# A four-layer decoder on one core: the expert router of layer 2 picks its 64 tokens by quarters and numbers them with matmuls

## What is computed

```python
xf = x.reshape(n_tokens, d)                       # 1024 x 128
rms = jnp.sqrt(jnp.mean(xf * xf, axis=-1, keepdims=True) + EPS)
xn = xf / rms * norm_weight
logits = xn @ router_weight.T + router_bias       # 1024 x 16
probs = jax.nn.softmax(logits, axis=-1)
_, idx = jax.lax.top_k(logits.T, top_k)           # 16 x 64, top_k = 1024 / 16
xe = xn[idx]
h = jnp.einsum('ecd,efd->ecf', xe, fc1_weight) + fc1_bias[:, None, :]
h = jax.nn.gelu(h, approximate=False)
y = jnp.einsum('ecf,edf->ecd', h, fc2_weight) + fc2_bias[:, None, :]
gates = jnp.take_along_axis(probs.T, idx, axis=1)
flat_idx = idx.reshape(-1)
contrib = (y * gates[:, :, None]).reshape(-1, d)
output = jnp.zeros((n_tokens, d), dtype=x.dtype).at[flat_idx].add(contrib)
gate_sums = jnp.zeros((n_tokens, 1), dtype=x.dtype).at[flat_idx].add(gates.reshape(-1, 1))
```

## Time and profile before

| | us |
|---|---|
| runs before | 1656.31, 1650.27, 1657.39 |
| median | 1656.31 |
| profiled execution, its own time | 1656.52 |
| its span in the trace | 1654.7 |
| PE busy | 1475.0 (89%) |
| DVE busy | 993.3 (60%) |
| ACT busy | 675.9 (41%) |
| POOL busy | 394.5 (24%) |

### The profile page before, as it was taken

One profiled execution on the slowest core, in us unless ns is written; L12 is line 12 of the kernel. 1 busy time (PEld: TensorE's weight loads), 2 busy tenths in 40 slices (PEclk: granted clock), 3 DMA queues, 4 the chain that ended last, 5 costly groups with the idle time before them and its releaser, 6 DMA issues. The chain is left out here.

```text
span 1654.7 us, 25517 instructions
## 1 busy us (share of the span) xinstructions
PE 1475.0 (89%) x9683; PEld 914.8 (55%) x9683; DVE 993.3 (60%) x1912; ACT 675.9 (41%) x1656; POOL 394.5 (24%) x403
## 2 busy tenths in 40 slices
PE   8998999999999998987898948849999999997786
PEld 5665566544555566566685726634446666652334
DVE  5676383433466545456567357689887775664455
ACT  3675252233366635343311243415556666620002
POOL 3000031000101010005503033357785553300000
PEclk8999899999799999999898978989999999999999
DMA  2000001410000000000030302011010101379990
GB/s 89 2 2 2 3 1 47 160 38 25 15 1 2 2 16 1 9 10 4 1 125 18 98 10 75 2 39 33 31 52 14 25 15 20 65 173 233 230 209 13
DMA packets 18933, 78.98 MB, mean 48 GB/s; under 512 B 3912, under 2 KB 5750, under 8 KB 14336
## 3 DMA queue, kind: packets, MB, share of 16 engines
q1 hardware_dynamic: 18816, 77.40, 17.7%
HBM read 72.11 MB, written 1.08 MB: 44 GB/s over the span
## 5 line engine op out<-in xcount | busy, mean ns | idle before, releaser
L193 PE MATMUL psum<-ident 128*128 128x128 f32 x1360 | 180.6, 290 | 55.5 <-DVE wide L2108 20.9
L193 PEld LDWEIGHTS psum<-ident 128*128 128x128 f32 x1360 | 169.1, 203 | 74.5 <-DVE wide L2108 21.5
L184 POOL TENSOR_TENSOR rstd<-var,minus_half 128x4 f32<-128x4 f32 x30 | 30.6, 1021 | 621.4 <-DVE var L143 583.0
L510 DVE TENSOR_REDUCE quad_max<-psum 128x1 f32<-128x128 f32 (+3 forms) x256 | 113.5, 485 | 96.4 <-PE psum L403 96.2
L472 ACT ACTIVATE pt<-psum,quad_max 128x128 f32<-128x128 f32 (+3 forms) x256 | 133.3, 524 | 84.9 <-DVE quad_max L510 81.4
L2594 PE MATMUL psum<-pt,slots 128*128 128x512 f32 x256 | 125.0, 641 | 28.5 <-DVE pt L2732 28.5
L2573 PE MATMUL psum<-slots,xn_t 128*128 128x512 f32 x256 | 113.2, 602 | 19.6 <-DVE pt L2719 19.6
L2323 ACT ACTIVATE p<-psum,duo_max 128x512 f32<-128x512 f32 x128 | 86.7, 683 | 64.1 <-DVE duo_max L2358 61.8
L2594 PEld LDWEIGHTS psum<-pt,slots 128*128 128x128 f32 x256 | 50.4, 204 | 102.2 <-issue 51.4
L2358 DVE TENSOR_REDUCE duo_max<-psum 128x1 f32<-128x512 f32 x128 | 82.3, 684 | 36.8 <-PE psum L2245 36.6
L419 PE MATMUL psum<-ident,pt 128*128 128x128 f32 x640 | 91.8, 288 | 8.4 <-DVE p L527 7.3
(11 more groups left out here) (466 smaller groups left out, 2944.1 us busy)
## 6 DMA issues: line engine op xcount, KB each, us to landing
pt<-scratch_out_gates SPq DMA_DIRECT2D x32, 512.0 KB, 15.6
heads<-scratch_out_gates SPq DMA_DIRECT2D x32, 512.0 KB, 10.8
slots<-in_s_l0f SPq DMA_DIRECT2D x8, 514.0 KB, 3.6
wide<-scratch_gates SPq DMA_DIRECT2D x8, 512.0 KB, 6.9
slots<-in_s_l3v SPq DMA_DIRECT2D x8, 512.0 KB, 3.6
slots<-in_s_l3o SPq DMA_DIRECT2D x8, 512.0 KB, 5.8
weights<-in_w_l1a SPq DMA_DIRECT2D x1, 2624.0 KB, 9.6
slots<-in_s_l2f SPq DMA_DIRECT2D x4, 578.0 KB, 4.4
```

What stands on the lines that cost most here:

```text
L193: nc.tensor.matmul(m.ps[bank][:, 0:P], m.ident[:, :], m.ident[:, :], start=True, stop=True, skip_group_check=True)
L510: nc.vector.tensor_reduce(m.quad_max[:, n % 2, g:g + 1], m.ps[g][:, 0:keys], AX.X, ALU.max, negate=True).then_inc(m.quad_negmax, 1)
```

## The change

The router's product now gives four quarters of 256 tokens, each on its own group of 32 partitions (16 experts and 16 rows of zero weights, which the host adds), so that `logits` is 128 x 256. The 64 largest are found in two rounds of eight `max` and seven `match_replace`: first in each quarter, on all 128 partitions at 256 numbers each, giving `lists`; then four copies bring the four lists beside each other on partitions 0 to 15 (16 x 256), and the same search there gives the limit. It is written out 128 wide (`limit_wide`), PE turns it, and each partition, now a token, has the 16 limits beside its 16 logits (`token_logits`, which ACT has copied out of PSUM).

DVE compares: `above_bf` and `level_bf`, 128 tokens x 8 tiles x 16 experts in bfloat16. The running sums over tokens become products: `count_to` multiplies the mask with `up_to`, a triangle of ones, which counts within a tile, and adds the earlier tiles by seven products with `ones_sq`, a square of ones. Eight more products with `ones_sq` give the number above the limit. DVE decides which level ones are taken and adds them to `above_bf`; a second `count_to` gives the places, already with tokens on partitions. The copy of `places` goes away, as do the scans. POOL makes `ones_sq` and `up_to` at the head of its part of the stage.

The maximum over experts and the subtraction for the softmax now stand behind the two comparisons. The 115 matmuls of `keep_busy` become 48, and 3, 5 and 6 more at three later places.

```diff
@@ l2_ffn_tensor
-    for j in range(2):
-        bank = fill(m, pe, f"l2fr{j}")
-        nc.tensor.matmul(bank[0:E2, :], w["router"], m.xn_t[:, j * S:(j + 1) * S], start=True,
-                         stop=True).then_inc(filled(m, f"l2fr{j}"), 1)
-    for name, src in (("l2fl0", m.logits), ("l2fp0", m.places)):
-        if name == "l2fl0":
-            for j in range(2):
-                copied(m, pe, f"l2fr{j}")
-        else:
-            keep_busy(nc, m, 115)
-            pe.wait_ge(m.places_ready, 1)
-        bank = fill(m, pe, name)
-        for t in range(NT):
-            last = nc.tensor.transpose(bank[:, t * E2:(t + 1) * E2], src[0:E2, t * P:(t + 1) * P], m.ident[0:E2, 0:E2])
-        last.then_inc(filled(m, name), 1)
+    bank = fill(m, pe, "l2fr0")
+    for c in range(4):
+        last = nc.tensor.matmul(bank[32 * c:32 * c + 32, 0:QUARTER], w["router"], m.xn_t[:, c * QUARTER:(c + 1) * QUARTER],
+                                start=True, stop=True)
...
+    copied(m, pe, "l2fr0")
+    bank = fill(m, pe, "l2fl0")
+    for half in range(2):
+        at = slice(half * P, (half + 1) * P)
+        last = nc.tensor.transpose(bank[:, at], m.logits[:, at], m.ident[:, :])
+    last.then_inc(filled(m, "l2fl0"), 1)
+    keep_busy(nc, m, 48)
+    pe.wait_ge(m.router_limit, 1)
+    bank = fill(m, pe, "l2fp0")
+    nc.tensor.transpose(bank[:, 0:E2], m.limit_wide[0:E2, :], m.ident[0:E2, 0:E2]).then_inc(filled(m, "l2fp0"), 1)
+    keep_busy(nc, m, 3)
+    pe.wait_ge(m.masks_ready, 1)
+    pe.wait_ge(m.up_to_done, 3)
+    bank = fill(m, pe, "l2fc0")
+    count_to(nc, m, bank, m.level_bf)
+    for t in range(NT):
+        last = nc.tensor.matmul(bank[:, P:P + E2], m.ones_sq[:, :], m.above_bf[:, t, :], start=False, stop=t == NT - 1,
+                                skip_group_check=True)
+    last.then_inc(filled(m, "l2fc0"), 1)
+    keep_busy(nc, m, 5)
+    pe.wait_ge(m.masks_ready, 2)
+    bank = fill(m, pe, "l2fd0")
+    count_to(nc, m, bank, m.above_bf).then_inc(filled(m, "l2fd0"), 1)
+    keep_busy(nc, m, 6)
...
+def count_to(nc, m, bank, mask):
+
+    last = nc.tensor.matmul(bank[:, 0:P], m.up_to[:, :], mask[:, :, :].rearrange("p t e -> p (t e)"), start=True, stop=False,
+                            skip_group_check=True)
+    for t in range(NT - 1):
+        rest = NT - 1 - t
+        last = nc.tensor.matmul(bank[:, (t + 1) * E2:P].rearrange("p (n e) -> p n e", e=E2), m.ones_sq[:, :],
+                                mask[:, t:t + 1, :].broadcast_to([P, rest, E2]), start=False, stop=t == NT - 2,
...
@@ l2_ffn_vector
-    src = m.logits[0:E2, :]
-    for r in range(CAP // 8):
-        d.done(nc.vector.max(m.top8[0:E2, r % 2, :], src))
-        if r < CAP // 8 - 1:
-            d.done(nc.vector.match_replace(m.left[0:E2, :], m.top8[0:E2, r % 2, :], src, -BIG))
-            src = m.left[0:E2, :]
...
-    d.done(nc.vector.tensor_tensor_scan(count, one, level, 0.0, ALU.mult, ALU.add))
...
+    copied(m, dve, "l2fr0")
+    largest(m.logits[:, 0:QUARTER], m.left[:, 0:QUARTER], m.lists[:, 0, :])
+    for c in range(4):
+        last = nc.vector.tensor_copy(m.places[0:E2, c * CAP:(c + 1) * CAP], m.lists[32 * c:32 * c + E2, 0, :])
+    d.done(last)
+    largest(m.places[0:E2, 0:QUARTER], m.left[0:E2, 0:QUARTER], m.lists[0:E2, 1, :])
+    nc.vector.tensor_copy(m.limit_wide[0:E2, :], m.lists[0:E2, 1, CAP - 1:CAP].broadcast_to([E2, P])).then_inc(m.router_limit, 1)
...
+    nc.vector.tensor_tensor(m.level_bf[:, :, :], logits, each(bank[:, 0:E2]), ALU.is_equal)
+    d.done(nc.vector.tensor_tensor(m.above_bf[:, :, :], logits, each(bank[:, 0:E2]), ALU.is_gt))
...
+    nc.vector.engine_nop().then_inc(m.masks_ready, 1)
...
+    d.done(nc.vector.tensor_scalar(m.needed[:, :], bank[:, P:P + E2], -1.0, float(CAP), ALU.mult, ALU.add))
...
```

More of the change, by code:

```diff
@@ L1766 @@
 CAP = T // E2
+QUARTER = T // 4
 EXPERT_LAG, EXPERT_SLOTS = 3, 8
@@ L1861, in l2_ffn_scalar @@
     turn_scalar(nc, act, m, "l2fn")
[L1862 to L1865, removed]
+    bank = read(m, act, "l2fr0")
+    nc.scalar.activation(m.logits[:, 0:QUARTER], bank[:, 0:QUARTER], ACT.Identity,
+                         bias=w["router_b"]).then_inc(emptied(m, "l2fr0"), 1)
+    bank = read(m, act, "l2fl0")
+    nc.scalar.activation(m.token_logits[:, :, :].rearrange("p (c h) e -> p c h e", h=2),
+                         bank[:, 0:2 * P].rearrange("p (h c e) -> p c h e", h=2, c=4)[:, :, :, 0:E2], ACT.Copy).then_inc(emptied(m, "l2fl0"), 1)
     act.wait_ge(m.router_less_max, 2)
@@ L1915, in l2_ffn_vector @@
[L1915 to L1918, removed]
-    d.done(nc.vector.tensor_tensor_scan(count, one, level, 0.0, ALU.mult, ALU.add))
-    d.done(nc.vector.tensor_scalar(count, count, m.needed[0:E2, 1:2], None, ALU.is_le))
@@ L1921, in l2_ffn_vector @@
[L1921 to L1926, removed]
-    last16 = lambda ap: ap.rearrange("p (t o) -> p t o", o=1).broadcast_to([P, NT, E2])
-    bank = read(m, dve, "l2fl0")
-    logits = bank[:, 0:NT * E2].rearrange("p (t e) -> p t e", e=E2)
@@ L1930, in l2_ffn_vector, with largest @@
-    d.done(nc.vector.tensor_reduce(m.per_token[:, 1, :], logits, AX.X, ALU.max))
-    nc.vector.tensor_tensor(probs, logits, last16(m.per_token[:, 1, :]), ALU.subtract).then_inc(emptied(m, "l2fl0"), 1)
[L1932 to L1937, removed]
+    def largest(src, left, lists):
+        for r in range(CAP // 8):
+            top = lists[:, 8 * r:8 * r + 8]
+            d.done(nc.vector.max(top, src))
+            if r < CAP // 8 - 1:
+                d.done(nc.vector.match_replace(left, top, src, -BIG))
+                src = left
@@ new lines, in l2_ffn_vector @@
+    last16 = lambda ap: ap.rearrange("p (t o) -> p t o", o=1).broadcast_to([P, NT, E2])
+    each = lambda ap: ap.rearrange("p (o e) -> p o e", o=1).broadcast_to([P, NT, E2])
+    by_tile = lambda ap: ap.rearrange("p (t e) -> p t e", e=E2)
+    copied(m, dve, "l2fl0")
+    bank = read(m, dve, "l2fp0")
+    nc.vector.tensor_tensor(m.level_bf[:, :, :], logits, each(bank[:, 0:E2]), ALU.is_equal)
+    d.done(nc.vector.tensor_tensor(m.above_bf[:, :, :], logits, each(bank[:, 0:E2]), ALU.is_gt))
+    nc.vector.engine_nop().then_inc(emptied(m, "l2fp0"), 1)
@@ new lines, in l2_ffn_vector @@
+    nc.vector.engine_nop().then_inc(m.masks_ready, 1)
+    d.done(nc.vector.tensor_reduce(m.per_token[:, 1, :], logits, AX.X, ALU.max))
+    d.done(nc.vector.tensor_tensor(probs, logits, last16(m.per_token[:, 1, :]), ALU.subtract))
+    nc.vector.engine_nop().then_inc(m.router_less_max, 2)
+    bank = read(m, dve, "l2fc0")
+    d.done(nc.vector.tensor_scalar(m.needed[:, :], bank[:, P:P + E2], -1.0, float(CAP), ALU.mult, ALU.add))
+    nc.vector.tensor_tensor(m.place[:, :, :], by_tile(bank[:, 0:P]), each(m.needed[:, :]), ALU.is_le).then_inc(
+        emptied(m, "l2fc0"), 1)
@@ new lines, in l2_ffn_vector @@
+    copied(m, dve, "l2fc0")
+    d.done(nc.vector.tensor_tensor(m.level_bf[:, :, :], m.level_bf[:, :, :], m.place[:, :, :], ALU.mult))
+    nc.vector.tensor_tensor(m.above_bf[:, :, :], m.above_bf[:, :, :], m.level_bf[:, :, :], ALU.add).then_inc(m.masks_ready, 1)
+    bank = read(m, dve, "l2fd0")
+    dve.wait_ge(m.masks_ready, 2)
+    nc.vector.tensor_tensor(m.place[:, :, :], by_tile(bank[:, 0:P]), m.above_bf[:, :, :], ALU.mult).then_inc(
+        emptied(m, "l2fd0"), 1)
+    copied(m, dve, "l2fd0")
@@ L2957, in build @@
         m.ones_row = sb("ones_row", [1, P])
-        m.logits, m.left, m.places, m.running = m.q_t, m.k_t, m.o_t, heads[:, 0, :]
+        m.logits, m.left, m.places = m.q_t, m.k_t, m.o_t
         m.probs16 = sb("probs16", [P, NT, E2])
@@ L2961, in build @@
         m.gla_past = sb("gla_past", [P, NQ, H])
-        m.top8 = sb("top8", [P, 2, 8])
-        m.needed = sb("needed", [P, 2])
+        m.lists = sb("lists", [P, 2, CAP])
+        m.limit_wide = sb("limit_wide", [E2, P])
+        m.token_logits = sb("token_logits", [P, NT, E2])
+        m.above_bf = sb("above_bf", [P, NT, E2], BF16)
+        m.level_bf = sb("level_bf", [P, NT, E2], BF16)
+        m.up_to = sb("up_to", [P, P], BF16)
+        m.ones_sq = sb("ones_sq", [P, P], BF16)
+        m.needed = sb("needed", [P, E2])
         m.ones_col = sb("ones_col", [P, 1])
```

23 lines of the change are left out of this document (15 added, 8 removed).

## The result

| | before | changed |
|---|---|---|
| median of 4 runs, us | 1656.85 | 1643.44 |
| lowest to highest | 1650.27 to 1664.12 | 1634.52 to 1648.99 |
| profiled execution, its own time | 1656.52 | 1648.99 |
| its span | 1654.7 | 1646.9 |
| ratio of the two kernels, 95% interval | | 0.989 (0.9855 to 0.993) |

Three more series of the changed kernel, each against runs of the kernel before on the same chip, gave 0.9915 (0.9886 to 0.9945), 0.9892 (0.9864 to 0.9919) and 0.9908 (0.9877 to 0.9939). The mean of the four ratios is 0.990: some 16 us of 1660. The forecast was 1640.5, with 1635.5 to 1647. Three single executions that took 2252 to 7858 us (one of `fill_66`, two of the kernel before) are left out of medians and ratios.

A forecast was written before the change was run, and what follows sets the result against it. The program was taken as a chain through PE, which here waits for DVE's search. `wide` 13.1 us earlier plus 3.0 in the gathering made 16.1, from 1656.52 to 1640.5 us; range 1635.5 to 1647.

The forecast's parts named there:

- The start: Router's product to DVE's search: four overlapping products take 0.55 us, search starts after 1.27 in place of 2.69, saving 1.4.
- The search: DVE's top-64 search: two rounds of 7.15 us in place of one of 19.16, with 0.75 for copies between.
- rival 4: In the search, `max` and `match_replace` cost by the instruction, so rounds stay 19.16 us each; total 1666.5, chance 0.04.
- The clock: PE idles 3.8 us before the limit, its clock falls near 863 and is full again after about 3.5 us.
- Rival 1: PE's clock stays low into the gathering, most of its 3.0 us stay lost; gain 12.6 us, 1644, chance 0.21.
- Rival 2: PE's clock does not fall before the limit; gain 17.5 us, 1639, chance 0.10.
- eleven of eleven: All eleven PE idle stretches longer than 2.6 us in the trace end with a clock fall, so one was expected here.
- From the limit to the first `wide`: Turn, comparisons, counts and fillers between limit and `wide`: 6.25 us; 7.4 all at low clock, 4.9 all at full.
- The term for the first count: Sixteen bfloat16 matmuls after the comparisons: 1.9 us with the low clock, plus 0.3 for the result to reach DVE.
- the five fillers ahead of the second count: Idle matmuls on PE nearly fit beside DVE's four short operations, delaying the second count by 0.15 us.
- Rival 5: The new DVE-PE-DVE chain costs twice 6.25 us with the clock low throughout; gain about 7, 1649.5, chance 0.03.
- Rival 3: Later low-clock stretches fall elsewhere, each worth up to 1.7 us of PE time; 1637 to 1644, no separate chance.

The follow-up runs named there:

- fill_66: Changed kernel with 66 idle matmuls in place of 48 ahead of the wait for the limit; medians 1644.5 and 1645.2 us, ratios 0.9890 and 0.9889 to the kernel before.
- no_fill: Changed kernel without any of its 62 idle matmuls; 1653.7 us, ratio 0.9945 to the kernel before.
- halves: Changed kernel searching two groups of 512 tokens in place of four quarters, with 55 idle matmuls for 48 ahead of the limit; ratio 0.9927 to the kernel before.
- fill_200: Changed kernel with 200 idle matmuls in place of 48 ahead of the wait for the limit; median 1668.2 us, ratio 1.0054 to the kernel before.
- counts_only: Changed kernel with the old router's product and search, 65 idle matmuls ahead of the limit; medians 1645.5 and 1646.4 us, ratios 0.9914 and 0.9893 to the kernel before.

## Why the prediction held, and where its working did not

**The start.** 1.2 us from product to search, forecast 1.27. The four products overlap: 0.64 us, forecast 0.55. PE is not idle ahead of them, so the 0.2 us allowed for entering the groups were not needed.

**The search.** Rounds of 7.35 and 7.16, forecast 7.15 each; copies 0.78, forecast 0.75; the limit at +16.7, forecast 16.6. The reductions, of 128 and 1024 numbers with 256 between them, gave the right price for an instruction that no row showed at that length, and rival 4 (a price by the instruction) is dead. The reason given for taking 7.15, that three quarters of the slope come from rows at just these lengths, has no row behind it; 256 was read off the line between the two. The Trainium skill's formula ("VectorE: DVE Perf Modes", section "The TRN2 errata"), written for another operation, gave 424 ns; measured were 416 and 428. The section's advice of 512 numbers or more would have been wrong to follow here: `halves` has 512 in its first round and its stretch is 2.0 us longer.

**The clock.** It fell at the limit, as forecast, 3.6 us into the 4.3 us that PE was idle (forecast 3.8). The step "I take about 3.5 us: back to full near 866.5" failed: it was low for 6.8 us, in all four profiles of the change. The other half of the claim held, since it was back before the gathering, which took 13.97 us. Rival 1 (low into the gathering) is out, and `no_fill` shows what it would have been: 16.0 us. Rival 2 (no fall) is what `fill_66` makes on purpose, and it is worth 2.1 us in the stretch where 1.35 were reckoned. Its "eleven of eleven" was the luck of that trace. Over all fourteen, every one of the 42 idle stretches of PE above 4 us had a fall by 1.5 us behind its end, but 26 of the 123 between 2.6 and 4 us had none, the longest 3.85 us in `no_fill`. The 2.68 us in the next stage ended with a fall in the trace that the forecast was made from, and in none of the change. With 3.8 us forecast, the fall was less certain than it was called; 4.3 us came.

**From the limit to the first `wide`.** 5.8 us, forecast 6.25, and that closeness is luck. The step that failed is the price of the small products, together with that of the idle matmuls between them. The term for the first count was sized wrong: 1.9 us for 16 bfloat16 matmuls at the low clock, and 0.3 for the way back. Measured from the first one's start, DVE goes on after 0.94 us at the low clock (871.13 to 872.07) and 0.67 at full (870.40 to 871.07). The row of L403 with its 0.15 us each was a bad measure, since other matmuls stood between its pairs; the lower end, 0.05 behind one another, was the right one. With the clock low throughout, my own sum would have said 7.4, and with it at full 4.9, where 5.8 and 3.7 were measured. So the clock was taken 1.15 us too kindly (6.25 for 7.4) and the operations 1.6 us too dear (7.4 for 5.8), and the two nearly cancelled. Inside the second there is an error the other way: the five fillers ahead of the second count were to cost 0.15 us and cost 0.95 (1.00 us from the masks to the count, 0.05 in `fill_66`).

**The gathering and what is beside the path.** 3.0 us gained, as forecast. DVE waits 2.64 us for the first expert, forecast 2.7. POOL's three small operations end before its next work is due, which waits 17.31 us for DVE.

**The sum.** 16.1 us forecast, 16.4 in the stretch, 16 in the mean of the ratios; the first series alone gave 13.4. From the median before, 16.1 us less make 1640.2, not 1640.5. Rival 5 (the new chain costs twice 6.25) is out: it cost 5.8. That the program follows the stretch was argued from who waits for whom; the 60.2 us in all profiles show it up to the next stage, and `fill_200` bears it out for the total within its width. Rival 3, that the low stretches behind shift and take or give some, is real: the next stage is 1.2 us shorter in the change (46.4 for 47.6), and takes 2.8 us more in `fill_66`. The forecast's range, 1635.5 to 1647, was about as wide as the spread of the runs themselves.

Open is the total of `counts_only`, level with the change though 5.3 us behind in the stretch, and the total of `no_fill`, 7 to 9 us behind it though 0.4 behind in the stretch; of the latter 2.9 are the next stage's, 49.3 for 46.4.

## What to carry to other kernels

A top-k by rounds of eight on few partitions is worth splitting over idle partitions, since the price goes by the numbers in a row; by the measured price the best split makes the first round and the round over the candidates equally long (256 and 256 here; 512 and 128 were slower, 128 and 512 were not run). Look past the search, though: the running sums and the turning behind it were two thirds of the gain, once triangular products with tokens on the partitions had replaced them. And where a chain of small products hands over between two engines, count the idle matmuls ahead of each wait twice: too few lower the clock, and those that then run at the low clock come late themselves (here 1.6 of the 2.1 us between the change and `fill_66`).
